# A table lookup on GpSimd beside a transformer block: conversion of the indices, product buffers and waits

## What is computed

```python
def _ghost_linear(x, idx, lut):
    w = lut[idx]
    return jnp.einsum('bsh,oh->bso', x, w)
gate = _ghost_linear(x, gate_idx, lut)   # idx 688 x 256, int32, 0..15
up = _ghost_linear(x, up_idx, lut)       # idx 688 x 256
h = jax.nn.silu(gate) * up
return _ghost_linear(h, down_idx, lut)   # idx 256 x 688
```

## Time and profile before

| | us |
|---|---|
| median of 3 runs | 1378.33 (1376.38 to 1378.66) |
| the profiled execution | 1382.27 |
| its span (first to last instruction) | 1380.5 |
| PE busy | 1231.5 (89%) |
| DVE busy | 962.3 (70%) |
| ACT busy | 707.0 (51%) |
| POOL busy | 552.5 (40%) |

### The profile page before, as it was taken

The page is one execution under the profiler, slowest core; times in us unless marked ns, Lnnn a source line. Parts: engine busy times, 40 slices in busy tenths (PEclk is TensorE's granted clock), DMA queues, the critical chain, the costliest instruction groups (busy, mean ns, idle before and its releaser), DMA issues.

```text
span 1380.5 us, 24347 instructions
## 1 busy us (share of the span) xinstructions
PE 1231.5 (89%) x7708; PEld 946.4 (69%) x7708; DVE 962.3 (70%) x2821; ACT 707.0 (51%) x1639; POOL 552.5 (40%) x509
## 2 busy tenths in 40 slices
PE   6889888886469999999989999999998999999998
PEld 5435454443447787777877877778786788777787
DVE  5766777765467868778778678686677676675553
ACT  3354645455336456465464565554564654645442
POOL 0200000000038988898889888887802200000000
PEclk9799898888579999999999999999999999999999
DMA  6411011001110002101102001012001100000000
GB/s 216 123 30 46 24 43 55 24 32 62 61 55 23 32 11 101 41 0 41 41 10 91 21 27 39 8 38 96 4 30 62 34 32 23 8 0 1 16 16 31
DMA packets 31893, 56.85 MB, mean 41 GB/s; under 512 B 7096, under 2 KB 23328, under 8 KB 31312
## 3 DMA queue, kind: packets, MB, share of 16 engines
q1 hardware_dynamic: 27696, 42.93, 9.3%
q0 software_dynamic: 2976, 8.90, 2.2%
q10 hardware_dynamic: 1152, 4.19, 0.8%
HBM read 44.23 MB, written 11.66 MB: 40 GB/s over the span
## 4 chain that ended last, share of the span: by engine, by line
PE 54%; DVE 29%; issue 9%; ACT 5%; DMA 1%; SPq 1%; DVEq 0%; ACTq 0%
PE bank L1364 11%; PE bank L1342 7%; PE bank L278 6%; PE bank L280 6%; PE bank L279 6%; DVE qkst L1022 5%; DVE qk L1041 4%; PE bank L1353 4%; PE bank L1332 2%; DVE negmax L968 2%; PE bank L1277 2%; PE bank L1246 2%; DVE negmax L1054 2%; ACT hN L326 2%; PE bank L1264 1%
## 5 line engine op out<-in xcount | busy, mean ns | idle before, releaser
L574 POOL TENSOR_SCALAR gtmp<-gidx,lut 128x344 f32<-128x344 int32 (+2 forms) x210 | 302.8, 1442 | 21.3
L577 POOL TENSOR_TENSOR gacc<-gacc,gtmp 128x344 f32<-128x344 f32 (+2 forms) x210 | 183.4, 874 | 17.5
L1342 PE MATMUL bank<-kT,qT 128*128 128x128 f32 (+3 forms) x512 | 179.8, 442 | 9.4 <-ACT probs L776 9.4
L1364 PE MATMUL bank<-pT,v 128*128 128x128 f32 x1280 | 155.5, 277 | 12.3 <-ACT pT L769 12.3
L776 ACT ACTIVATE probs<-bank,negmax 128x128 f32<-128x128 f32 (+3 forms) x256 | 135.6, 530 | 53.6 <-DVE negmax L1054 50.9
L1054 DVE TENSOR_REDUCE negmax<-bank 128x1 f32<-128x128 f32 (+3 forms) x256 | 123.6, 485 | 54.9 <-PE bank L1343 53.5
L1364 PEld LDWEIGHTS bank<-pT,v 128*128 128x128 f32 x1280 | 148.0, 192 | 16.2 <-DVE oL L1064 14.9
L968 DVE TENSOR_REDUCE negmax<-bank 128x1 f32<-128x512 f32 (+3 forms) x176 | 108.9, 636 | 67.5 <-PE bank L1266 66.6
L1022 DVE BATCH_NORM_STATS2 qkst<-qk 128x6 f32<-128x128 f32 x512 | 110.2, 281 | 61.7 <-issue 61.6
L278 PE MATMUL bank<-wgH,hL 128*128 128x512 f32 x384 | 152.9, 398 | 0.2 <-issue 0.2
L280 PE MATMUL bank<-wgH,hH 128*128 128x512 f32 x384 | 153.0, 399 | 0.0
(11 more groups left out here) (215 smaller groups left out, 2707.2 us busy)
## 6 DMA issues: line engine op xcount, KB each, us to landing
hH<-h_saved SPq DMA_DIRECT2D x16, 512.0 KB, 3.8
hL<-h_saved SPq DMA_DIRECT2D x16, 512.0 KB, 4.8
qst<-q_parts SPq DMA_DIRECT2D x96, 64.0 KB, 2.3
wg<-in_wqkv SPq DMA_DIRECT2D x4, 1536.0 KB, 8.3
gate<-gates POOLq DMA_DIRECT2D x4, 512.0 KB, 7.0
wo<-in_wo SPq DMA_DIRECT2D x4, 512.0 KB, 9.1
out<-x SPq DMA_DIRECT2D x8, 256.0 KB, 2.1
wmod<-in_wmod SPq DMA_DIRECT2D x1, 1536.0 KB, 10.7
```

What stands on the lines that cost most here:

```text
L574: link(pool.tensor_scalar(tmp if j else acc, part, float(j), lut1[0:rows, j:j + 1], ALU.is_equal, ALU.mult))
L577: link(pool.tensor_tensor(acc, acc, tmp, ALU.add))
L1342: pe.matmul(bank[SCORE_BANKS[i % 3]][:, 0:n], qT[:, h, t * P:n], kT[:, h, 0:n], start=True, stop=False)
L1364: last = pe.matmul(bank[7][:, t * P:(t + 1) * P], v1[:, k, h * HD1:(h + 1) * HD1], pT1[:, h % 2, at:at + P], start=(k == 0), stop=(k == t))
```

## The change

Per job the indices are converted to f32 once (`gidf`), and the comparisons read this copy. The products go to three buffers in turn (`gtmp`), and product j + 1 is issued ahead of addition j, so that an addition waits for the addition before it and for a product two instructions back, and a product waits for the addition that read its buffer, two instructions back. Indices (`gidx`) and accumulators (`gacc`) have two buffers each: the load of job i + 1 is issued once job i's indices are in, before job i's operations, and a job waits for the store of the job two before. The number of comparisons (16 a job) and additions (15) is as before; 14 copies are new. All of it stays on POOL.

```diff
-        gidx = sb(sg1, "gidx", [P, PIECE], I32)
-        gacc = sb(sg1, "gacc", [P, PIECE])
-        gtmp = sb(sg1, "gtmp", [P, PIECE])
+        gidx = sb(sg1, "gidx", [P, 2, PIECE], I32)
+        gidf = sb(sg1, "gidf", [P, PIECE])
+        gacc = sb(sg1, "gacc", [P, 2, PIECE])
+        gtmp = sb(sg1, "gtmp", [P, 3, PIECE])
...
-            def link(ins):
+            def mark(ins):
                 n[0] += 1
                 ins.then_inc(gat, 1)
-                pool.wait_ge(gat, n[0])
+                return n[0]
...
+            def load_job(i):
+                src, rows, cols, at = jobs[i]
+                pool.dma_start(gidx[0:rows, i % 2, 0:cols], src).then_inc(loaded_idx[i % 2], 16)
+
+            load_job(0)
+            pool.wait_ge(loaded_lut, 16)
             for i, (src, rows, cols, at) in enumerate(jobs):
-                part, acc, tmp = gidx[0:rows, 0:cols], gacc[0:rows, 0:cols], gtmp[0:rows, 0:cols]
-                pool.dma_start(part, src).then_inc(loaded_idx, 16)
-                pool.wait_ge(loaded_idx, (i + 2) * 16)
-                if i:
-                    pool.wait_ge(gat_dma, i * 16)
-                if rows < P:
-                    link(pool.memset(gacc[:, 0:cols], 0.0))
-                for j in range(LUT):
-                    link(pool.tensor_scalar(tmp if j else acc, part, float(j), lut1[0:rows, j:j + 1],
-                                            ALU.is_equal, ALU.mult))
-                    if j:
-                        link(pool.tensor_tensor(acc, acc, tmp, ALU.add))
-                pool.dma_start(wffn_saved[:, at:at + cols], gacc[:, 0:cols]).then_inc(gat_dma, 16)
+                part, acc = gidf[0:rows, 0:cols], gacc[0:rows, i % 2, 0:cols]
+                tmp = [gtmp[0:rows, k, 0:cols] for k in range(3)]
+                pool.wait_ge(loaded_idx[i % 2], (i // 2 + 1) * 16)
+                if i + 1 < len(jobs):
+                    load_job(i + 1)
+                if i >= 2:
+                    pool.wait_ge(gat_dma[i % 2], i // 2 * 16)
+                cleared = mark(pool.memset(gacc[:, i % 2, 0:cols], 0.0)) if rows < P else 0
+                pool.wait_ge(gat, max(n[0], cleared))
+                converted = mark(pool.tensor_copy(part, gidx[0:rows, i % 2, 0:cols]))
+                pool.wait_ge(gat, converted)
+                added = [mark(pool.tensor_scalar(acc, part, 0.0, lut1[0:rows, 0:1], ALU.is_equal, ALU.mult))]
+                made = mark(pool.tensor_scalar(tmp[1], part, 1.0, lut1[0:rows, 1:2], ALU.is_equal, ALU.mult))
+                for j in range(1, LUT):
+                    ready = made
+                    if j + 1 < LUT:
+                        if j >= 3:
+                            pool.wait_ge(gat, added[j - 2])
+                        made = mark(pool.tensor_scalar(tmp[(j + 1) % 3], part, float(j + 1), lut1[0:rows, j + 1:j + 2],
+                                                       ALU.is_equal, ALU.mult))
+                    pool.wait_ge(gat, max(added[-1], ready))
+                    added.append(mark(pool.tensor_tensor(acc, acc, tmp[j % 3], ALU.add)))
+                pool.wait_ge(gat, added[-1])
+                pool.dma_start(wffn_saved[:, at:at + cols], gacc[:, i % 2, 0:cols]).then_inc(gat_dma[i % 2], 16)
```

More of the change, by code:

```diff
@@ L369, in build @@
         norm_f1 = Norm("norm_f1", 3, hN, hF, sm)
-        loaded_c, loaded_w0, loaded_x, loaded_idx, loaded_misc = map(
-            sem, ("loaded_c", "loaded_w0", "loaded_x", "loaded_idx", "loaded_misc"))
+        loaded_c, loaded_w0, loaded_x, loaded_lut, loaded_misc = map(
+            sem, ("loaded_c", "loaded_w0", "loaded_x", "loaded_lut", "loaded_misc"))
+        loaded_idx = [sem(f"loaded_idx{i}") for i in range(2)]
         loaded_m0, loaded_m, loaded_x0, consts, q_hi, k_hi = map(
@@ L388, in build @@
         h1_stored = sem("h1_stored")
-        gat, gat_dma = sem("gathered"), sem("gathered_dma")
+        gat, gat_dma = sem("gathered"), [sem(f"gathered_dma{i}") for i in range(2)]
         w1_loaded, w1_hi, w1_lo, h1_loaded, gqk_ready = map(
@@ L550, in _ @@
             n = [0]
-            def link(ins):
+            def mark(ins):
                 n[0] += 1
                 ins.then_inc(gat, 1)
-                pool.wait_ge(gat, n[0])
-            pool.dma_start(lut1[:, :], a["lut"].to_broadcast([P, LUT])).then_inc(loaded_idx, 16)
+                return n[0]
+            pool.dma_start(lut1[:, :], a["lut"].to_broadcast([P, LUT])).then_inc(loaded_lut, 16)
             jobs = [(a[f"idx_{w}"][k * P:(k + 1) * P, o:o + PIECE], P, PIECE, n * KT * INTER + k * INTER + o)
@@ L582, in _ @@
             pool.wait_ge(h1_stored, NB * 32)
-            pool.wait_ge(gat_dma, len(jobs) * 16)
+            for k in range(2):
+                pool.wait_ge(gat_dma[k], (len(jobs) + 1 - k) // 2 * 16)
             pool.memset(f32(wguH[:, :, :, INTER:]), 0.0).then_inc(f_zero, 1)
```

## The result

The changed kernel took 1385.11 us against 1377.38 us, medians of 7 runs each; the ratio is 1.0055, 95% interval 1.0041 to 1.0069, so +5.6 to +9.5 us. It is slower, by some 5 to 8 us.

A forecast was written before the change was run, and what follows sets the result against it. PE, busy 89% of the span, heads the chain. Denser POOL blocks, +0.75 us in 9.5 rounds = +7 us, less 1.9 us for freed rounds, made +5 us: 1383.5 us, 8-in-10 range 1376 to 1404 us.

The forecast's parts named there:

- The lookup is off the path and acts on DVE alone: POOL's 600 us lookup ends 50 us before its use; it delays DVE, costing some 27 us of the path.
- 0.65 us a block for an addition, 0.23 us for a comparison: Delay of DVE's small steps beside POOL's operations; 0.88 us lost per pair of comparison and addition.
- A slack of 2.2 us a round, used up: DVE's spare time before a middle round's first maximum, 2.2 us, already gone beside the lookup, so added delay is paid in full.
- The comparison unchanged on f32: POOL's comparison of 344 columns, 1.57 us on int32, was taken to last as long on f32.
- 56 us off the lookup through waits that are two back: POOL's operations wait two back, saving 0.13 us at each of some 430 hand-overs: 56 us off the lookup.
- signs named beforehand: Signs of being right, among them additions starting before the comparison ends, lookup ending near 924 us, small steps 6.5 us.
- +0.75 us a round in 9.5 rounds, -1.9 us for the rounds freed: Rounds beside the lookup: denser POOL blocks cost +7 us, rounds freed by a shorter lookup return 1.9 us; +5 us in all.
- +0.4 us a round that was forecast: DVE's 17 small steps in a round beside the lookup lengthen by 0.4 us as POOL's operations stand closer.
- term for the multiplications (+2.4 us): DVE's multiplications and additions to x beside the lookup lengthen by +0.25 us a round over 9.5 rounds.
- freed rounds (-1.9 us): The lookup ending 75 us earlier frees 1.4 of the last, lighter rounds, worth some 1.9 us.
- The rival with a faster comparison: POOL's f32 comparison gets shorter, so blocks crowd DVE more: +10 to +34 us, 1388 to 1412 us; chance 0.33.
- The rival that a shorter lookup frees its rounds: Blocking of DVE falls with the lookup's length: -4 to -11 us, 1367 to 1374 us; chance 0.12.

The follow-up runs named there:

- e5_short: The changed kernel with 2 comparisons and 1 addition a job in place of 16 and 15 (wrong weights); 1353.14 us, ratio 0.9822 against the kernel before.
- e8_tree: The changed kernel with 16 product buffers, all 16 comparisons of a job first, then the additions as a tree; ratio 1.0041 against the kernel before.
- e6_all_compare: The changed kernel with each addition replaced by a comparison (wrong weights); 1358.08 us, ratio 0.9843 against the kernel before.
- e4: e3_half_waits with job i also waiting for DVE's multiplications and, except in first rounds, additions to x in round i; 1356.28 us.
- e7: e4 with loading and splitting of the weight strips also held until DVE's additions to x in round 14; 1351.85 us, ratio 0.9792.
- e3_half_waits: The changed kernel without the wait ahead of each product; ratio 1.0028 against the kernel before.
- e10: e3_half_waits with the comparisons made with j modulo 4 (wrong weights); ratio 1.0061 against the kernel before.
- e1: The kernel before with only indices loaded a job ahead, two index pieces and accumulators, stores waited for two jobs later; ratio 1.0000.

## Why the prediction was right, point by point

- *The lookup is off the path and acts on DVE alone*: right. e5_short takes 24 us off the kernel by shortening work that nobody waits for.
- *0.65 us a block for an addition, 0.23 us for a comparison*: right for the addition (0.85 - 0.19 us in e8_tree), a little low for the comparison (0.23 to 0.32 us), and it is what decides: e6_all_compare has more work and hardly any loss.
- *A slack of 2.2 us a round, used up*: right; it comes back as DVE's wait for PE in e4 and e6 (0.84 and 0.71 us) and whole in e5 (2.2 us). In e4 and e7 the small steps still take 5.1 to 5.5 us in rounds 1 to 3 and 5 to 7, and those rounds cost nothing for it.
- *The comparison unchanged on f32*: right, 1.43 us. That the comparison takes its input in the first third of its time, the reason given, was read from what it costs DVE and not shown. The Trainium skill, "GPSIMD: programming the Q7 cores", section SBUF Data Layout, sends every element through float32 on the read port; the trace agrees as far as it can, with 1.44 us on int32 and 1.43 us on f32.
- *56 us off the lookup through waits that are two back*: wrong, and with it two of the signs named beforehand, additions that start ahead of the comparison's end and a lookup that ends near 924 us. Only the first five hand-overs behind a job's conversion closed, and the lookup was 34 us shorter instead of 75: 32 us of pauses at loads (one of them had been 7.1 us, ahead of the last job) and some 9 us of gaps, less some 8 us for the conversions. The error was to read the gap of 0.08 to 0.10 us as the price of a wait on the instruction ahead for all operations alike, from two operations at the kernel's start that differ in more than this. For the comparisons with 0 to 3 it was so: they have the gap before and none after. In e3_half_waits half of these waits are gone and the gap stays, and in e8_tree 16 comparisons follow without any wait, with 0.093 us ahead of each from the fifth on.
- *+0.75 us a round in 9.5 rounds, -1.9 us for the rounds freed*: +7 - 1.9 = +5 us were forecast; 5.2 and 7.6 us were measured, and the twelve rounds say 5.6 us. The small steps gave the +0.4 us a round that was forecast (5.63 to 6.03), but that number was luck. It was worked out from 0.26 us less between all operations, most of which stayed. In e10, where they did close, the small steps rose by another 0.6 us a round over the changed kernel. What made them longer here was, by the traces, the closed pauses, which the sum counted only as length off the lookup and not as density. In rounds 4 and 8 the steps rose by 1.78 and 1.36 us: without a pause none of the eleven rounds has short small steps, where before rounds 4 and 8 had 4.54 and 5.09 us because a pause fell into them. As e1's time shows hardly any loss, how much is the pauses' and how much the new order's is open. The multiplications gave nothing (92.7 us in rounds 0 to 14 in both). PE's clock, worth some 1 us, was in no term. The freed rounds gave next to nothing: rounds 9 and 10 together are 0.2 us shorter (105.1 us against 105.3). So the term for the multiplications (+2.4 us) and that for the freed rounds (-1.9 us) were both mis-sized, in opposite directions, and the sum came out near because of that. The direction was no luck: denser additions and a slack that is used up are what e10 and e4 show.
- *The rival with a faster comparison* fell with the first row. *The rival that a shorter lookup frees its rounds* fell with e10_small_numbers: 65 us shorter, 8.4 us slower.

What stays open: why e1_loads_ahead, whose rounds beside the lookup look like the changed kernel's, was timed at 0 with 2 us to either side, and whether the length of round 12 belongs to a kernel or to one execution.

## What to carry to other kernels

Work on GpSimd that nobody waits for can still set the time, through VectorE: look in both engines' timelines for a VectorE step that takes 0.85 us beside a GpSimd operation and 0.19 us elsewhere. Packing such work closer makes it worse, and where it stands matters more than how long it is: a wait on a semaphore that VectorE already counts, so that GpSimd pauses while VectorE is on the path, gained 28 us here, where the tuned order of GpSimd's own work lost 5 to 8. Delay spread over many rounds is absorbed by each one's slack; delay in one piece is not (e8_tree's profile, a round of 59.2 us). Look at the granted clock beside the round that was delayed: a late VectorE can lower it.

## What the runs showed of the hardware that was not expected

- A GpSimd comparison of 128x344 (1.44 us) holds up VectorE's steps by only 0.23 to 0.32 us, at its start; an addition of two inputs (0.92 us) by 0.65 us. A chain of VectorE steps beside additions in a row advances by one step per addition (0.85 us a step in e8_tree).
- Where PE stood idle for 2.10 us, its granted clock was 0.50 just afterwards; in the same place of the kernel before it stood idle for 1.74 us and kept 1.00.
- Of GpSimd's operations with an immediate number to compare with, those with 0 to 3 followed the operation ahead without a gap once they no longer waited for it, those from 4 on had 0.093 to 0.10 us ahead and, with an addition next, 0.08 us behind, whether they wait or not and whatever they multiply with. With j modulo 4 no gap was left in any of 14 jobs (the lookup 32 us shorter than in e3); with eighths half of them stayed, from 5/8 on. In e10 only this argument changed; what makes the difference inside the engine is open.
